# Another order for the four engine programs of a four-layer attention and feed-forward kernel, up to the end of the attention loop's lead-in

## What is computed

```python
x = x + tanh(g_xattn[0]) * L0_xattn(layernorm(x), ctx, ...)      # energy, softmax, x_m = logits @ attention^T
x = x + tanh(g_ffn[0])   * L0_ffn(layernorm(x), gate_w, down_w, ...)
x = x + tanh(g_xattn[1]) * L1_xattn(layernorm(x), ctx, ...)
x = x + tanh(g_ffn[1])   * L1_ffn(layernorm(x), ...)

def bit_linear(x, w, g):                        # L0_ffn, twice: gate/up (256 -> 2 x 704), down (704 -> 256)
    xn = rms_norm(x, g)
    xq = ste(xn, activation_quant(xn))          # round(x * 127 / max|x|), one scale for each token
    wq = ste(w, weight_quant(w))                # round(w / mean|w|) to -1, 0, 1
    return xq @ wq.T
h = gate * sigmoid(gate) * up

q, k = rmsnorm(x @ Wq), rmsnorm(ctx @ Wk)       # L1_xattn, 16 heads of 128
out = softmax(q k^T * scale) @ (ctx @ Wv) @ Wo
```

## Time and profile before

| | us |
|---|---|
| median of 3 runs | 615.18 (615.14 to 615.51) |
| the profiled execution | 616.09 |
| its span, first to last instruction | 614.3 |
| PE busy in the span | 603.3 (98%) |
| DVE, ACT, POOL busy | 477.9, 422.7, 236.7 |

### The profile page before, as it was taken

One profiled execution on the slowest core, in us unless ns is written; L12 is line 12 of the kernel. 1 busy time (PEld: TensorE's weight loads), 2 busy tenths in 40 slices (PEclk: granted clock), 3 DMA queues, 4 the chain that ended last, 5 costly groups with the idle time before them and its releaser, 6 DMA issues.

```text
span 614.3 us, 11619 instructions
## 1 busy us (share of the span) xinstructions
PE 603.3 (98%) x3644; PEld 522.6 (85%) x3644; DVE 477.9 (78%) x1139; ACT 422.7 (69%) x1082; POOL 236.7 (39%) x282
## 2 busy tenths in 40 slices
PE   8979999999999999999999999999999999999997
PEld 6757899999999999999998888888887888887886
DVE  3999988987777787688876787788777676777776
ACT  6999999888888888889897344465444444443442
POOL 5999998576665566656662020000000000000000
PEclk9999999999999999999999999999999999999999
DMA  8513202000000000000030545453856466545640
GB/s 299 196 53 102 95 11 78 2 2 2 2 2 2 1 2 2 1 2 1 11 121 3 170 147 154 129 171 96 216 156 167 116 176 175 156 154 149 195 128 34
DMA packets 33653, 56.47 MB, mean 92 GB/s; under 512 B 12800, under 2 KB 13504, under 8 KB 33600
## 3 DMA queue, kind: packets, MB, share of 16 engines
q1 hardware_dynamic: 33312, 55.82, 30.4%
q10 hardware_dynamic: 288, 0.00, 0.0%
HBM read 53.45 MB, written 1.31 MB: 89 GB/s over the span
## 4 chain that ended last, share of the span: by engine, by line
PE 89%; DVE 5%; ACT 4%; issue 1%; POOL 1%; DVEq 0%; ACTq 0%; POOLq 0%
PE bank L310 25%; PE bank L312 25%; PE bank L311 25%; PE bank L985 4%; PE bank L960 2%; PE bank L952 2%; DVE hs L2088 1%; PE bank L912 1%; PE bank L1026 1%; PE bank L829 1%; DVE attT_lo L2182 1%; PE bank L835 1%; ACT att L1575 1%; ACT w L1478 1%; PE bank L815 1%
## 5 line engine op out<-in xcount | busy, mean ns | idle before, releaser
L1623 ACT ACTIVATE inter_hi<-inter 128x512 fp32r<-128x512 f32 x63 | 39.8, 632 | 140.5 <-DVE inter L2287 140.5
L310 PE MATMUL bank<-xnT_hi,front_hi 128*128 128x512 f32 (+1 forms) x260 | 102.0, 392 | 0.0
L312 PE MATMUL bank<-xnT_hi,front_lo 128*128 128x512 f32 (+1 forms) x260 | 101.7, 391 | 0.0
L311 PE MATMUL bank<-xnT_lo,front_hi 128*128 128x512 f32 (+1 forms) x260 | 101.6, 391 | 0.0
L2291 DVE TENSOR_TENSOR inter_lo<-inter,inter_hi 128x512 fp32r<-128x512 f32 x63 | 43.6, 692 | 37.9 <-ACT inter_hi L1623 37.3
L1575 ACT ACTIVATE att<-bank,shift,rq 128x256 f32<-128x256 f32 x128 | 71.3, 572 | 0.0
L596 POOL TENSOR_TENSOR att<-att,rowinv 128x512 f32<-128x512 f32 x60 | 63.1, 1067 | 11.1 <-DVE rowinv L2187 11.1
L2260 DVE TENSOR_TENSOR prod<-gate_s,bank 128x512 f32<-128x512 f32 x63 | 43.3, 687 | 21.6 <-PE bank L312 19.5
L2170 DVE TENSOR_REDUCE rowmax<-bank 128x2 f32<-128x512 f32 x64 | 43.6, 686 | 20.7 <-PE bank L312 20.4
L311 PEld LDWEIGHTS bank<-xnT_lo,front_hi 128*128 128x128 f32 x260 | 48.9, 188 | 11.3
L312 PEld LDWEIGHTS bank<-xnT_hi,front_lo 128*128 128x128 f32 x260 | 48.8, 188 | 11.3
(11 more groups left out here) (273 smaller groups left out, 1811.7 us busy)
## 6 DMA issues: line engine op xcount, KB each, us to landing
w_all<-w_rows SPq DMA_DIRECT2D x128, 128.0 KB, 3.0
raw<-in_expert_w SPq DMA_DIRECT2D x32, 384.0 KB, 3.5
wvo_raw<-in_expert_w SPq DMA_DIRECT2D x16, 384.0 KB, 3.5
e_more<-in_expert_w SPq DMA_DIRECT2D x16, 384.0 KB, 3.6
raw<-in_head_qk SPq DMA_DIRECT2D x8, 384.0 KB, 3.1
wvo_raw<-in_head_vo SPq DMA_DIRECT2D x4, 384.0 KB, 3.8
w_keep<-in_head_vo SPq DMA_DIRECT2D x4, 384.0 KB, 3.3
gate_raw<-in_gate_wT SPq DMA_DIRECT2D x2, 704.0 KB, 9.0
```

What stands on the lines that cost most here:

```text
L310: pe.matmul(out, l_hi, r_hi_, start=start, stop=False, skip_group_check=True)
L311: pe.matmul(out, l_hi, r_lo_, start=False, stop=False, skip_group_check=True)
L312: return pe.matmul(out, l_lo, r_hi_, start=False, stop=stop, skip_group_check=True)
L1623: act.activation(inter_hi[:, slot, :], inter[:, slot, :], ACT.Copy).then_inc(a_Ihi, 1)
```

## The change

All four lists are written in another order. No call is added or taken away, no bank is changed, and SP's program is the same. PE's list has in addition 14 more lines of waits (234 against 220); most of the added ones wait for PE's own counters (t_abs, t_oA, t_y1, t_z1, t_T and others) and stand in front of a wait that already follows from it. Line numbers of ACT and DVE helpers are 14 higher in the changed file. The diff has some 500 changed lines; two short pieces, then the rows that show the order at three places.

```diff
@@ PE
+            pe.wait_ge(t_oA, 2)
             pe.wait_ge(v_xA, 2)
             keep_busy(0, 8)
+            sum_abs([2], 5)
+            turn_att(2, 4)
             turn_q1(0, 0)
-            pe.wait_ge(a_x0, 3)
+            fuse_vo(0, 6)
+            pe.wait_ge(a_q1, 1)
+            up_0(0)
+            gate_0(0)
             turn_q1(1, 7)
...
@@ DVE
-            low_w(0)
             inv_max_1(1)
             round_down()
             scales_1(1)
+            low_w(0)
+            round_1(2)
             times_up_0(0)
...
```

More of the change, by code:

```diff
@@ L646, in _ @@
             times_gain(1)
+            low_ctx()
             root_2(0)
-            low_ctx()
+            times_gain(2)
             scale_back_1(2)
+            root_1(3)
+            limit_1(2)
             power_2(0)
-            limit_1(2)
-            times_gain(2)
             rms_k(0)
-            root_1(3)
-            power_1(3)
             times_gain(3)
             scale_back_2(0)
-            scale_back_1(3)
+            power_1(3)
             limit_2(0)
             root_2(1)
-            times_rk(0)
+            times_gain(4)
@@ L1207, in _ @@
             turn(0, 0)
+            pe.wait_ge(v_xB, 7)
+            proj_q(4, 5, True)
+            pe.wait_ge(a_rawK, 5)
+            turn(0, 1)
+            pe.wait_ge(t_T, 1)
+            pe.wait_ge(v_Tlo, 1)
+            turn_rows_1(1, 2)
+            pe.wait_ge(v_xB, 8)
+            turn_q(2, 7)
             pe.wait_ge(a_exp, 6)
             turn_k(3, 0)
-            pe.wait_ge(a_rawK, 5)
-            turn(0, 1)
-            pe.wait_ge(a_Mhi, 8)
             proj_q(5, 6, True)
-            pe.wait_ge(v_Qlo, 3)
-            turn_q(3, 7)
-            pe.wait_ge(v_Tlo, 1)
-            turn_rows_1(1, 2)
             values(0)
-            pe.wait_ge(v_Klo, 4)
-            pe.wait_ge(a_exp, 8)
-            scores(2)
+            pe.wait_ge(t_u, 2)
             pe.wait_ge(c_u, 2)
             turn(1, 0)
+            turn_q(3, 7)
+            pe.wait_ge(t_TK, 4)
+            pe.wait_ge(v_Klo, 4)
+            scores(2)
             turn(1, 1)
-            pe.wait_ge(v_Qlo, 4)
-            turn_rows_1(2, 7)
+            pe.wait_ge(t_T, 3)
+            pe.wait_ge(v_Tlo, 3)
+            proj_k(5, 2, True)
             pe.wait_ge(a_sqQ, 20)
@@ L2311, in _ @@
             norm_A(0)
+            stats_0(2)
             inv_A(1)
-            stats_0(2)
+            norm_A(1)
             aggr_0(2)
+            inv_A(2)
             stats_0(3)
-            norm_A(1)
+            norm_A(2)
+            add_A(0, 1)
             aggr_0(3)
-            inv_A(2)
-            max_A(3, 3)
-            add_A(0, 1)
-            norm_A(2)
-            weight_scale(0, 0, 2 * INTER * HID)
-            inv_scale(0)
             stats_1(0)
             aggr_1(0)
+            weight_scale(0, 0, 2 * INTER * HID)
             times_g1(0)
             times_g1(1)
+            inv_scale(0)
+            max_A(3, 3)
+            absmax_1(0)
             add_A(1, 0)
-            absmax_1(0)
             stats_1(1)
-            weight_scale(1, 5, INTER * HID)
+            aggr_1(1)
             inv_max_1(0)
-            aggr_1(1)
-            scales_1(0)
-            inv_scale(1)
+            inv_A(3)
             times_g1(2)
             times_g1(3)
+            scales_1(0)
             round_1(0)
-            inv_A(3)
-            round_1(1)
             norm_A(3)
             absmax_1(1)
-            low_w(0)
+            weight_scale(1, 5, INTER * HID)
+            inv_scale(1)
+            round_1(1)
             inv_max_1(1)
@@ L2351, in _ @@
             stats_1(2)
+            aggr_1(2)
             times_up_0(1)
-            aggr_1(2)
             times_g1(4)
             times_g1(5)
-            key_gain()
+            low_w(1)
             absmax_1(2)
             absmax_2(0)
+            times_up_0(2)
+            absmax_2(1)
             inv_max_1(2)
-            low_w(1)
+            add_A(3, 4)
             scales_1(2)
+            inv_max_2(0)
+            round_1(4)
+            stats_1(3)
             low_m(0, 6)
-            absmax_2(1)
@@ L2364, in _ @@
-            times_up_0(2)
-            round_1(4)
+            aggr_1(3)
             first_mean_k(0)
-            add_A(3, 4)
-            inv_max_2(0)
-            stats_1(3)
             times_up_0(3)
+            times_g1(6)
+            times_g1(7)
             scales_2(0)
-            aggr_1(3)
             round_1(5)
             round_2(0)
-            times_g1(6)
-            times_g1(7)
+            absmax_1(3)
+            absmax_2(2)
+            times_up_0(4)
+            inv_max_1(3)
@@ L2392, in _ @@
-            stats_2(1)
-            first_mean_k(1)
+            aggr_2(1)
+            low_m(1, 7)
             scales_2(1)
-            aggr_2(1)
-            absmax_2(4)
             round_2(2)
             times_up_0(6)
-            low_m(1, 7)
+            low_w(2)
             round_2(3)
-            absmax_2(5)
-            low_w(2)
             times_up_0(7)
             low_rows(0, 0, 1)
+            add_down(2, 5)
+            absmax_2(4)
+            absmax_2(5)
+            inv_max_2(2)
@@ L2405, in _ @@
+            low_k(0, 0)
+            stats_2(2)
+            scales_2(2)
+            round_2(4)
+            first_mean_k(1)
+            round_2(5)
             absmax_2(6)
[L2406 to L2408 removed]
+            absmax_2(7)
+            add_down(3, 3)
+            aggr_2(2)
             low_w(3)
[L2410 to L2415 removed]
+            mean_q(0)
```

490 lines of the change are left out of this document (240 added, 250 removed).

## The result

The changed kernel takes 619.09 us (median of 4 runs, 619.06 to 619.47) against 615.35 us (615.14 to 615.74) for the kernel before on the same chip. The ratio is 1.0062, 95% interval 1.0044 to 1.0079. So it is slower by 3.7 us where 0.5 was forecast, and it lies outside the range of 613.1 to 617.5. The profiled execution has a span of 617.3 us against 614.3. The loss is 0.6%, three times what a measurement of this kernel can tell from no change, and most of it lies in one stretch.

A forecast was written before the change was run, and what follows sets the result against it. PE, busy 98% of the span, was taken as the bound, with idle holes mostly before 57 us. First mark +0.2, second mark +0.3 and loops 0 summed to +0.5 us: 615.18 to 615.7, range 613.1 to 617.5.

The forecast's parts named there:

- Softmax, weight scale, gates: From 8 us to turn_gate(1) near 23.5 us: reordered softmax, layer norm, weight scale and gate rounding cost 0.
- keep_busy: PE near 21.6 us waits about 0.7 us for add_A(1); price 0 to 0.4, +0.2 taken at silu_0(0).
- First gate times up: times_up_0(0) on DVE comes later because scales_1(1) ahead of it waits for POOL's power_1(1); +0.9 taken.
- the second branch: At times_up_0(0): DVE's round_down holds POOL up, power_1(1) ends at 28.3, times_up_0(0) at 29.6, 1.2 late.
- the first branch: At times_up_0(0): POOL not held up, power_1(1) ends at 27.85, times_up_0(0) at 29.2, 0.8 late.
- the walk: The forecast's method: new lists stepped through call by call, using starts and lengths from the old trace.
- rival 1: POOL's second-pair chain idles DVE near 27 us; first mark 1.3 to 2.5 late, 616.5 to 617.8; chance 0.20.
- The tiles behind: Later L0 feed-forward tiles: times_up_0(2), (7) earlier, (3), (5) later than before; PE idles 1.5 us ahead of turn_q1(4).
- First mark: Start of the first query projection, proj_q(0): 57.25 to 57.4 against 57.18 us; +0.2, between -0.7 and +1.2.
- Second mark: End of the lead-in at 126 us: PE stays full from the first projection on; +0.3, between -0.5 and +1.5.
- Loops: The loops behind 126 us are unchanged and PE-bound: 0.
- The second: Rival: PE not full from 57 to 126 us, two or three waits of 0.5; 616.5 to 617.3; chance 0.06.

The follow-up runs named there:

- experiment 10: Changed kernel with fuse_vo(4) moved back ahead of turn_rows_1(0) on PE: 619.24 us, ratio 1.0055 to the kernel before.
- Experiment 5: Changed kernel, order kept, products of k in mean_k(3) to mean_k(6) replaced by one-input maxima (output differs): 615.94 us, ratio 1.0007 to the kernel before.
- 6: Kernel before with products of k in mean_k(3) to mean_k(6) replaced by one-input maxima (output differs): 615.68 us, ratio 1.0001.
- 7: Changed kernel with three wide POOL products replaced by equally long powers over 128x4 (output differs): 614.93 us, late distance 69.22, loops 484.2 instead of 487.
- 12: Kernel before with mean_k(6) moved ahead of low_o(2) on DVE: 617.86 us; same move with one-input products in mean_k(3) to mean_k(6): 616.85 us.
- 1: Changed kernel with mean_k(6) moved from between the two row_max of pair 4 to behind row_shift(4) on DVE: 619.07 us, ratio 1.0051.
- 2: Changed kernel with mean_k(6) moved behind row_shift(4) and mean_k(3) ahead of row_max(0, 0) on DVE: 618.19 us, ratio 1.0042.
- 11: Changed kernel with mean_k(3) ahead of row_max(0, 0), mean_k(6) behind row_shift(4), split_m(3) behind low_att(2, 1) on DVE: 618.05 us, ratio 1.0038.
- 13: Changed kernel with fuse_vo(4), mean_k(3), mean_k(6), split_m(3) moved and times_rk(3) to (6), normalise_att(0) to (5) as tensor_scalar on POOL: 617.01 us, ratio 1.0018.

## Why the prediction was wrong, point by point

Times in the changed profile stand 0.84 us earlier than in that of before at the first energy product (9.67 against 10.51); they are given here with that added.

- *Softmax, weight scale, gates.* weight_scale at 19.17 (19.2 forecast), mix(1) at 19.39 (19.4), the gates rounded at 23.24 (23.5), turn_gate(1) at 23.34 (23.55). Right.
- *keep_busy.* PE waited 0.50 ahead of it (0.7 forecast), turn_q1(0) came at 24.82 (24.9 to 25.1), silu_0(0) at 27.61 (27.7). Right.
- *First gate times up.* power_1(1) took 1.41 us instead of 0.89 beside DVE's round_down, so POOL was held up, as the second branch of that step had it. It still ended at 27.77, as the first branch had it (27.85), because it had started some 0.5 earlier than in the walk: two errors that cancel. DVE idled 0.66 (0.5); times_up_0(0) at 29.09 (29.2 to 29.6). The term is right, in part by luck, and rival 1 didn't come.

```profile
27.04 0.16 DVE L2071 SCALAR_TENSOR_TENSOR tinyB<-tinyB 128x2 f32<-128x2 f32 x1 [0.66 <-POOL tinyB L493]
```

- *The tiles behind.* times_up_0(2), (3), (5), (7) at 35.78, 40.32, 46.72, 54.11 against 36.3, 40.7, 47.2, 54.4: 0.3 to 0.5 early each. The gap ahead of turn_q1(4) was 1.16 (1.5), the clock did not fall. Right.
- *First mark.* 57.76 against 57.25 to 57.4, since the second of POOL's normalise_1 pair took 1.70 us instead of about 0.7 (half of 1.38), and PE waited for it. It ran from 51.9 to 53.6 us of the profile, beside low_w on DVE, whose two inputs lie in SBUF:

```profile
51.37 2.24 POOL L560 TENSOR_SCALAR u<-x,negm,rstd 128x256 f32<-128x256 f32 x2
```

```profile
51.91 0.94 DVE L2095 TENSOR_TENSOR front_lo<-raw,front_hi 128x768 fp32r<-128x768 f32 x1
```


```profile
53.76 0.63 PE L815 MATMUL bank<-ident,u 128*128 128x128 f32 x4 [0.95 <-POOL u L560]
```

  0.4 too low, the same kind of error as in the next step with the engines exchanged (that DVE caused it is read from the overlap, no run tests it). By experiment 10 it is of little weight: 0.86 us won there were worth 0.4 at the end.
- *Second mark.* **This is the step that failed.** It read: "In my walk its new order finds nearly every operand ready, with 0.5 to 2 us to spare", and took +0.3, between -0.5 and +1.5. The distance grew by 3.25. The operands were late because DVE was: the walk took every length from the old trace, so mean_k had its 1.2 us wherever the new list put it. In the new order four of its calls met wide work on POOL and took 2.81, 2.06, 1.83 and 3.19 us, split_m(3) 1.85 instead of 1.14. That is 5.8 us more of DVE in a stretch where it has 8.35 to spare, and mean_k(6), mean_k(5) and split_m(3) stood ahead of calls that PE waits for. Experiment 5 shows it from DVE's side and 6 is its control; 7 shows it from POOL's side, and 12 puts part of it into the kernel before. With the stretches gone the walk's claim holds: late 67.37, with no wait of PE.
- *The sum.* Both halves hang on one thing: the lengths of the old trace. The prediction did allow for POOL being held up by DVE at one place of the first half (0.4 between its two branches at times_up_0(0), of which it took 0.1), and never asked whether DVE could be held up by POOL in the second.
- *Loops.* 0 forecast, 0.0 measured (487.1 and 487.1).
- *Rivals.* The second had the right stretch and the wrong size: two or three waits of 0.5 at thin places; there were seven between 0.2 and 1.0. Of the signs, "PE busy over 68.3 of the 69 us" failed (67.01), and so did the limit of 1 us on PE's waits behind 57 us: they came to 1.8 in the profile's own count. The bound of +1.5 for the second mark came from the old lengths as well.

What stays open: how the late loss of the changed kernel divides among the stretched calls. The moves of experiments 1, 2 and 11 each gave 0.4 to 0.7 us of the late distance, and each moved the stretch as well as the call. Why mending by moves (13) recovers 2.0 us less of the late distance than the one-input form (5) was seen as new waits, and not traced further.

## What to carry to other kernels

When instructions are moved across engines' schedules, the length of an instruction is no constant: look up for each DVE instruction with two SBUF inputs what POOL will run beside it in the new order, and price it once with and once without that neighbour. Do the same for POOL's instructions: both steps that the walk had too short were of this kind. In the profile, an engine whose busy time rises while its count falls is a sign; group by line, compare the mean ns of the two kernels, and look at which neighbour's end the long ones share. And don't test a list by putting back one engine's order alone: the run measures a new head-of-line wait (9 us here), not the cause.
